# One-hot tiles of layer 0: six small VectorE instructions a step become one, and TensorE reads the tiles with a step of six elements

## The reference: what is computed

```python
s2 = concatenate([src, dst]); d2 = concatenate([dst, src]); ef2 = concatenate([ef, ef])
for l in range(3):
    e_in = concatenate([h[s2], h[d2], ef2], axis=-1)
    msg = leaky_relu(e_in @ We1[l]) @ We2[l]
    red = segment_sum(msg, d2, num_segments=3125)
    out = leaky_relu(concatenate([h, red], axis=-1) @ Wn1[l]) @ Wn2[l]
    h = out + h
x = layernorm(x + out)
```

## Time and profile before

| | us |
|---|---|
| median of 3 runs (4554.65 to 4555.74) | 4555.39 |
| the profiled execution's own time | 4540.66 |
| its span, first to last instruction | 4538.9 |
| TensorE matmul busy | 3134.0 (69%) |
| VectorE busy | 2927.2 (64%) |
| ScalarE busy | 2092.5 (46%) |
| sums L1151: 11232 matmuls, busy | 793.7 |
| one-hot tiles L892: 1872 instructions, busy | 330.8 |
| edge loop of layer 0 | from 1672 to about 2622 |
| edge loops of layers 1 and 2 | from about 2677 to 3550, and from about 3605 to 4480 |

### The profile page before, as it was taken

The page is one execution under the profiler, slowest core; times in us unless marked ns, Lnnn a source line. Parts: engine busy times, 40 slices in busy tenths (PEclk is TensorE's granted clock), DMA queues, the critical chain, the costliest instruction groups (busy, mean ns, idle before and its releaser), DMA issues.

```text
span 4538.9 us, 95215 instructions
## 1 busy us (share of the span) xinstructions
PE 3134.0 (69%) x28957; PEld 2255.1 (50%) x28958; DVE 2927.2 (64%) x7075; ACT 2092.5 (46%) x4052; POOL 780.5 (17%) x826
## 2 busy tenths in 40 slices
PE   3443443443442558888888879898888788988886
PEld 2111111111110556666666657777777577767774
DVE  7444444444443369999999966666666566666665
ACT  0000000000000346666666667777777677777774
POOL 0455555555555100000000000000000000000000
PEclk6555555555555779999999989999999899999998
DMA  6000000000000646666565624444444244444443
GB/s 176 4 5 5 5 5 5 5 5 5 5 5 5 147 123 212 207 213 209 207 215 204 214 102 162 162 154 163 153 159 157 86 164 152 164 152 159 157 155 112
DMA packets 191495, 533.07 MB, mean 117 GB/s; under 512 B 34359, under 2 KB 71958, under 8 KB 189430
## 3 DMA queue, kind: packets, MB, share of 16 engines
q1 hardware_dynamic: 163926, 517.51, 34.1%
q0 software_dynamic: 27552, 15.37, 1.8%
HBM read 375.40 MB, written 157.52 MB: 117 GB/s over the span
## 4 chain that ended last, share of the span: by engine, by line
PE 46%; DVE 10%; issue 9%; DMA 2%; ACT 1%; POOL 0%; DVEq 0%; SPq 0%; ACTq 0%; POOLq 0%
PE gath L1096 16%; PE sums L1151 12%; PE sums L1096 8%; PE gath L1089 5%; DVE loop_buf L875 3%; DVE loop_buf L892 2%; DVE big L806 2%; PE sums L1089 2%; DMA recc<-records 2%; PE sums L1001 1%; DVE gsel L810 1%; PE sums L1159 0%; PE sums L1021 0%; PE sums L1160 0%; PE sums L1165 0%
## 5 line engine op out<-in xcount | busy, mean ns | idle before, releaser
L806 DVE SCALAR_TENSOR_TENSOR big<-big 128x768 f32<-128x768 f32 (+1 forms) x957 | 907.7, 949 | 676.4 <-ACT big L593 635.0
L1096 PE MATMUL gath<-t_hi,gsel 128*128 x3744 | 944.9, 278 | 0.0
L1096 PE MATMUL gath<-t_lo,gsel 128*128 x3744 | 944.3, 278 | 0.0
L1151 PE MATMUL sums<-loop_buf 128*128 128x128 f16 x11232 | 793.7, 221 | 202.6 <-issue 202.0
L875 DVE TENSOR_TENSOR loop_buf<-big,loop_buf 128x768 f16<-128x768 f32 x936 | 889.7, 951 | 0.0
L507 POOL DMA_INDIRECT records<-rec,rowi x784 | 754.7, 963 | 630.7 <-DVE rec L747 391.2
L984 PE MATMUL sums<-t_lo,tri 128*128 128x326 f16 x784 | 345.5, 454 | 714.0 <-issue 480.2
L1151 PEld LDWEIGHTS sums<-loop_buf 128*128 128x128 f16 x11232 | 680.7, 99 | 311.0 <-issue 156.8
L725 DVE SCALAR_TENSOR_TENSOR gsel<-sums,t_lo 128x326 f32<-128x326 f32 x784 | 367.3, 496 | 724.0 <-remote 536.6
L597 ACT ACTIVATE loop_buf<-big 128x768 f16<-128x768 f32 x936 | 782.0, 836 | 1.9
L593 ACT ACTIVATE big<-gath 128x512 f32<-128x512 f32 x936 | 559.6, 598 | 356.8 <-PE gath L1096 356.8
(11 more groups left out here) (156 smaller groups left out, 2632.1 us busy)
## 6 DMA issues: line engine op xcount, KB each, us to landing
gsel<-gsel_d SPq DMA_DIRECT2D x208, 576.0 KB, 3.9
loop_buf<-ssel_d SPq DMA_DIRECT2D x208, 576.0 KB, 5.1
numb<-nums_d SPq DMA_DIRECT2D x106, 576.0 KB, 4.6
gsel_d<-gsel SPq DMA_DIRECT2D x104, 576.0 KB, 5.5
ssel_d<-loop_buf SPq DMA_DIRECT2D x104, 576.0 KB, 6.5
fchunk<-feat_d SPq DMA_DIRECT2D x313, 144.0 KB, 2.9
records<-rec,rowi POOLq DMA_INDIRECT x784
recc<-records POOLq DMA_DIRECT2D x30, 272.0 KB, 5.1
```

Source lines behind the costliest of these rows:

```text
L806: return dve.scalar_tensor_tensor(m, m, SLOPE, m, ALU.mult, ALU.max)
L1096: return pe.matmul(uv, gsel[:, h, (2 * tc + s) * P:(2 * tc + s + 1) * P], at[n], start=False, stop=n == 3, skip_group_check=True)
L1151: last = pe.matmul(out_n, m[:, place, w0:w0 + D], ssel[:, ts, s, :], start=False, stop=False, skip_group_check=True)
```

## The change

All six one-hot matrices of a step are made by one VectorE instruction. Its output is laid out as (node, tile and side), with the six (tile, side) values of one node side by side. Its inputs are a new constant tile `iota_k`, which holds each node number six times in a row and is made once ahead of the loop, and six neighbouring columns of `numcol`, read again for each node. `numc` with its copy and its two waits goes. The matmuls of the sums read column after column of one (tile, side) out of that layout, so the elements that they read lie six elements (12 bytes) apart, where they lay side by side before. This is so in all three layers, since layers 1 and 2 read back what layer 0 has written. Sizes of buffers and of transfers stay as they are.

```diff
-        ssel = loop_buf[:, 0:ssel_words].bitcast(F16).rearrange("p (t s e) -> p t s e", s=2, e=P)
+        ssel = loop_buf[:, 0:ssel_words].bitcast(F16).rearrange("p (q e k) -> p q e k", e=P, k=2 * STEP)
...
+        iota_k = sb("iota_k", [P, P, 2 * STEP], F16)
...
-        numc = sb("numc", [P, ITER * 2], F32)
...
-            then(dve.memset(ssel[:, SLOTS - STEP * LAG:SLOTS, :, :], 0.0))
+            then(dve.memset(ssel_part(1), 0.0))
+            then(dve.tensor_copy(iota_k[:, :, :], iota[:, 0:P].unsqueeze(2).to_broadcast([P, P, 2 * STEP])))
...
-                            dve.wait_ge(msg_set, step0 + AHEAD)
-                            dve.tensor_copy(numc[:, :], numcol[:, ds(it * (2 * ITER), 2 * ITER)]).then_inc(numc_set, 1)
-                            dve.wait_ge(numc_set, it + 1)
...
-                                for t in range(STEP * q, STEP * q + STEP):
-                                    for s in range(2):
-                                        last = dve.tensor_scalar(ssel[:, t % SLOTS, s, :], iota[:, 0:P],
-                                                                 numc[:, 2 * t + s:2 * t + s + 1], None, ALU.is_equal)
+                                nums = numcol[:, ds(it * (2 * ITER) + q * (2 * STEP), 2 * STEP)]
+                                last = dve.tensor_tensor(ssel[:, q % (2 * PART_STEPS), :, :], iota_k[:, :, :],
+                                                         nums.unsqueeze(1).to_broadcast([P, P, 2 * STEP]), ALU.is_equal)
...
-                                ts = (t + i - STEP * LAG) % SLOTS
+                                at_step = (q - LAG) % (2 * PART_STEPS)
...
-                                        last = pe.matmul(out_n, m[:, place, w0:w0 + D], ssel[:, ts, s, :], start=False,
+                                        last = pe.matmul(out_n, m[:, place, w0:w0 + D], ssel[:, at_step, :, 2 * i + s], start=False,
```

More of the change, by code:

```diff
@@ L288, in build @@
         ssel_kept = [sem(f"ssel_kept{h}") for h in range(2)]
-        numc_set = sem("numc_set")
         gath6_done = sem("gath6_done")
@@ L343, in ssel_part @@
         def ssel_part(h):
-            return ssel[:, h * PART:(h + 1) * PART, :, :].rearrange("p t s e -> p (t s e)")
+            return ssel[:, h * PART_STEPS:(h + 1) * PART_STEPS, :, :].rearrange("p q e k -> p (q e k)")
         NUM_AHEAD = 2
```

## The result

The changed kernel takes 5424.32 us (median of 4 runs, 5421.44 to 5429.38) against 4555.02 for the kernel before in the same series: slower by 869 us, a ratio of 1.1908 with a 95% interval of 1.1889 to 1.1927. The forecast was 4733 with a range up to 4970: the sign was right, the size far off.

The account below looks back on a forecast made before the run. VectorE was taken to bound layer 0 and TensorE layers 1 and 2. Terms of +164 us (layers 1 and 2) and +14 (layer 0) gave +178 on 4540.66, 4719; 14.7 more for the median made 4733 us, range 4485 to 4970.

Parts of the forecast that it names:

- Who owns the stages: Edge loops: VectorE sets layer 0's turn at 36.55 us, TensorE layer 1's at 33.60.
- VectorE's part: Layer 0: 11.8 us a turn removed, 12 new instructions of 0.24 to 0.87 us added; VectorE's turn 26.7 to 34.2.
- The price of a gap: Sums on TensorE, all layers: a matmul between 55.8 and 107 ns, middle 81, so 25 ns more each.
- The rule that was weighed: Sums' SBUF reads in 16-byte lines: 96 lines or 80 ns a matmul; it moved the chance, not the sum.
- What was given back: Layers 1 and 2: longer sums let ScalarE's clearing catch up, 0.5 us a turn x 52 = -26 us.
- Case A: Sums' gaps are free; layers 1 and 2 stand still, layer 0 gains 51 us: 4505 us; chance 0.37.
- D: VectorE's new instruction runs at one element a cycle; 4519 us with free gaps; chance within the 0.37 for those.
- B: Sums at half pace, 107 ns a matmul: +357 in layers 1 and 2, +110 in layer 0, 5022 us; chance 0.15.

Follow-up runs that it names:

- e4: Kernel before, a step's six VectorE instructions replaced by one writing the old layout, each number twice in numc: 4509.05 us against 4542.79, ratio 0.9927.
- e3: Kernel before without numc, a step's six VectorE instructions replaced by one writing the old layout, each number read 128 times in a row: 4527.35 us, ratio 0.9971.
- e5: Kernel before, the sums' moving operand read from a tile of zeros by steps of 1 to 32 elements: 5083.04 us against 4190.87.
- e1: Kernel before, with only the sums' reading changed to a step of six elements: 5409.08 us against 4542.79, ratio 1.1909.
- e2: Changed kernel, with the sums reading 128 neighbouring elements in place of every sixth: 4506.65 us against 4542.79, ratio 0.9923.
- e10: The same kernel as e4, run again on another chip: 4156.61 us against 4194.21 for the kernel before, ratio 0.9911.
- e8: e4 with layer 0's next features issued ahead of the three 576 KB transfers at three of four parts: 4140.95 us against 4194.21, ratio 0.9871.
- e7: Kernel before, the sums' stationary operand read from a tile of zeros by steps of 1 to 32 elements: 4204.36 us against 4190.87.
- e6: Kernel before, the sums' moving operand read from a tile of zeros in groups of neighbours at various distances: 4315.46 us against 4190.87.

## Why the prediction was wrong

*Who owns the stages.* Right. VectorE held layer 0 and TensorE layers 1 and 2, and the sums' longer time fell on the chain, where they now hold 35.9% of the whole span.

*VectorE's part.* Right within its bounds. The sum took 0.55 us from start to start, the middle of 0.24 and 0.87. Measured are 0.47 from start to start, as at 2150.93 us in e4, where the leaky relu starts at 2151.40; the recorded length is 551 ns. That the middle of two far bounds came so close was luck, and the forecast didn't hang on it. The copy that makes iota_k and the address arithmetic cost nothing that shows. The Trainium skill ("VectorE: DVE Perf Modes", the perf-mode tier table) gives this instruction two elements a cycle; the estimate of 0.47 us by that rule agrees with the trace. What the faster pace asks for is in e3 and e4: neighbours in the innermost dimension of every operand, two being enough.

*The price of a gap.* This is the step that failed. The text bound a matmul "above: one element delivered in the time that two take now", 107 ns, and called it half pace. Measured are 170 ns, outside both ends. The row behind that bound shows how fast the array goes at the 1.2 GHz level, with neighbours to read; it says nothing about how fast memory delivers. The bound was a statement on the array, put where one on the reading was needed. No row of the kernel before had a moving operand with gaps, and the honest upper end was open. The middle between a true end and a false one was 81 ns, and the range up to 102 ns a matmul inherited the mistake. The prediction did leave 0.15 to "half pace or beyond", but its terms had no mechanism by which a matmul could go beyond.

*The rule that was weighed.* The count of lines was right, 96 for a step of six, and it decides: with the price of a line that the text assumed, "as long as two columns do now", 0.83 ns, 80 ns come out; the price measured in e5 is 1.77 ns, 96 x 1.77 = 170. That is more than four columns' time at 2.4 GHz (0.42 ns each). A fetch that costs more than the columns it serves was in no term of the sum.

Where the Trainium skill ("SBUF — State Buffer", Specifications (TRN2)) asks for at least two hits on a line, the measurement differs: with two hits (step 4) a matmul takes 114 ns, twice as long as with neighbours, with 2.67 (step 3) 87 ns, and only four (step 2) were free. The note further down on that page (Door 1: The DMA port swizzle) that eight 16-bit elements may be strided over for free differs more: at a step of eight the matmul takes 226 ns.

*What was given back.* This term was mis-sized too, in the other direction. I took 0.5 us a turn. Twelve steps longer by 1.38 us make 16.6, but 24 turns of layer 1 in the changed kernel, each begun by its longest idle piece ahead of the sums, take 45.71 us each (most take 45.4 to 45.6; four take 46.9 to 47.0, and in these the gathers of the step behind the idle piece run at the 1.2 GHz level for some 3 us):

```profile
2981.07 2.22 PE L1146 MATMUL sums<-loop_buf 128*128 128x128 f16 x12 [0.62 <-issue]
...
4078.21 2.22 PE L1146 MATMUL sums<-loop_buf 128*128 128x128 f16 x12 [0.64 <-issue]
```

That is 12.1 more than 33.60, so 4.5 us a turn came back. TensorE's waits show which. In layer 1 before, 26 turns in 870 us:

```profile
PE sums L1151 <- issue: 67.9, 84, 1.4
PE sums L1089 <- issue: 29.8, 25, 1.3
```

In layer 1 after, 13 turns in 600 us:

```profile
PEld sums L1146 <- ACT sums L589: 15.1, 26, 0.9
PE sums L1146 <- issue: 8.3, 13, 0.6
```

The wait for ScalarE's clearing, the only one that the prediction counted, went from 1.6 us a turn (40.6 in all) to 1.15: some 0.4, close to its 0.5. The idle time in which TensorE waits for nothing that the profile shows went from 3.8 us a turn to 0.6, and that 3.1 the sum had left out. It lies mostly at a turn's end, where the address arithmetic of the next turn stands; that this is what the longer sums cover is a likely reading, not a shown one. The last 1.0 us isn't traced.

With 170 ns and these turns (45.71 in layers 1 and 2, 45.63 in layer 0) the prediction's sum is 52 x 12.1 for layers 1 and 2 and 26 x 9.1 for layer 0, 866 us; the layers together grew by 864.

*The rivals.* Case A (gaps free) is refuted by e1 and e5, but its mechanism, VectorE's freed time, is what e2 measures: 36 us where I had 51, and 15 where I had 36 for an instruction at that slower pace (e3). The waits keep more than the 1.0 us a turn over TensorE's 33.60 that I left them: 1.7 in e2, of which 0.6 goes when the features are issued first (35.2 in e10, 34.55 in e8). D is refuted by the 551 ns. B was the nearest, at 5022, and still 400 us short.

## What to carry to other kernels

A layout that lets one engine do six instructions in one is paid for by every engine that reads it, every time: here 312 steps were made cheaper by 0.5 us, and 11232 matmuls dearer by 114 ns. Count the 16-byte lines that a matmul's moving operand touches: with four columns to a line it was free. If a gap must be somewhere, try it on the stationary operand (free up to a step of seven, e7) or on VectorE's side, where pairs 68 bytes apart cost nothing that shows. When a resource has no row at all in the trace, its upper end is open: a bound taken from a neighbouring mechanism is none, and one small kernel that sweeps the size answers it.

## What the runs showed of the hardware

- TensorE's moving operand, float16, at the 2.4 GHz level: the times fit 1.77 ns for each new 16-byte line of a partition or 0.44 ns a column, whichever is more; at most one line a column, and 216 to 232 ns for 128 columns from a step of eight elements on (e5, e6).
- Which lines follow each other doesn't matter: pairs 8, 12 or 32 elements apart cost 114, 114 and 110 ns (e6).
- The stationary operand: steps up to seven elements free to within 2 ns, 60 to 63 ns a matmul in place of 56 from eight to sixteen (e7).
- VectorE's comparison of two float16 operands, 768 elements: 551 ns with neighbours innermost in all operands (the changed kernel), 552 with rows of only two neighbours (e4), 951 when one operand stands still along the innermost dimension (e3).
- 144 KB issued behind three transfers of 576 KB land in 6.3 us (e10), issued ahead of them in 2.9 (e8).
